# A two-layer kernel: staged first stores, remainders by identity products, attention stacks with spread rows

## The chip, the cores and the metric

The kernel runs on one core of a Trainium2 chip, in one launch. The time is that of the device, in microseconds, for one execution; the median over several runs is compared. The core has a matmul engine (PE, TensorE, with its weight loads PEld), a vector engine (DVE), an activation engine (ACT), a general engine (POOL) and a queue engine for transfers (SP). ACT and POOL can issue transfers too.

## The reference

`x` is (8, 256, 256). Two conditioned residual layers follow each other: `x = x + L0(x)`, then `x = x + L1(x)`.

```
L0: x*s1, layer norm over the channels; q, k, v = projections, each scaled per sample and channel (demodulation)
    16 heads of width 16: softmax(q k^T / 4) v, projected by w; plus v projected by u (skip); all float32
L1: xr, gate = x W_in^T (512 each); xr + t_emb; causal depthwise convolution of 4 taps; silu
    xn = layer norm of 512 channels;  Bm, Cm, dt = xn W_xproj^T (16 each)
    dt = tanh(dt W_dt^T + b_dt) * 0.01;  Ad = 1 - dt*tanh(A_log);  Bd = Bm * min(|xn|, 1)
    256 steps in time: h = clip(h*Ad + Bd x xn, -10, 10);  y = sum over d of C_d h_d
    out = ((y + D*xn) * silu(gate)) W_out^T
```

## The kernel before, in words

Five engine programs are written out by hand; semaphores order them. Every engine works through its own instructions in the order in which they stand, so a wait holds all that stands behind it. SP's queue is in order as well.

**Attention (0 to some 245 us).** Work goes sample by sample. For q and k of a sample PE projects the normalised `xnT` (L940), ACT copies the result to `qk` (L614) and POOL and ACT split it into three bf16 parts (`part`). `stack(b)` on SP (L287 and following) writes the parts of one sample to DRAM by eight transfers (L294) and reads them back as stacks `qst`, `kst` of 96 rows (partitions 0 to 95, by runs of 48, 32 and 16 rows; L307), so that one bf16 matmul of 96 rows gives all needed products of the parts. `max_scores` (L963) makes scores with queries on the partitions, DVE reduces them to row maxima `mx` (L1486), PE turns them round, ACT casts them to `mT` and issues a transfer of one row, `m_row`, into partition 96 of the q stack (L678), where the k stack holds -1. `scores` (L978) then multiplies 97 rows, and gives scores less their maximum, ready for ACT's Exp (L693); `weigh` (L993) multiplies with v. Stacks are in three buffers. PE's `sample(b)` interleaves the scores of sample b, the maxima of b + 1 and the projections of b + 2. Before the loop come the modulated statistics (DVE L1391, L1359), the demodulation sums (PE L924), and sample 0 and 1.

**Middle part (some 245 to 350 us).** Convolution, projections and layer norm statistics of layer 1. Then, for tiles (sample, half of time) in the order FINISHED, the first eight being the first half of each sample: DVE finishes a tile's `xn` by two passes (`centre` L1560, `scale` L1568); ACT casts it to bf16 (`leave_parts` L793); POOL subtracts the cast (`leave_first` L484, into `xrem`); ACT casts the remainder (`second_part` L807); POOL subtracts again into the third part (`leave_second` L490); ACT also squares the tile for the norms (L801). SP stores the parts to `xs_d` (`store_parts` L342). Meanwhile DVE makes the running products of Ad and their inverses (L1619 to L1628), PE turns them round, and `split` (L1635 to L1639) makes three parts of d and, when the norms are there, of B (bsplit). Those go to `bd_d` (`store_d`, `store_b` L263; twelve stores of B over both halves, 32-byte pieces). PE projects the gates 0 to 7 (`project_gate` L1164), ACT takes them through Silu (`take_gate` L765). The first slabs of x parts and B parts are read back into `xst` and `bst` (`load_x` L353, `load_b` L361) by SP, in slabs of 16 time steps, the first slab in two pieces of 8.

**Recurrence (350 us to the end).** 256 steps. PE makes `u` of one step by one bf16 matmul (L1280) in bank t % 4; DVE makes the clipped step by a custom instruction (L1664); PE sums states with C into y (`y_steps` L1291, banks 4 and 5), four steps at a time. Output of a slab, its gate and its projection follow one slab later, and so do the parts of tiles 8 to 15.

## Time and profile before

| | us |
|---|---|
| median of 3 runs (562.87 to 564.33) | 562.97 |
| the profiled execution | 563.17 |
| its span, first to last instruction | 561.4 |
| busy: PE / DVE / ACT / POOL | 471.6 / 430.0 / 253.5 / 194.0 |
| mean granted clock of TensorE | 0.948 |

The page lists what is busy and for how long; the chain of waits follows the work that ended last back through what released it; views by time show one engine's instructions with the idle time before them in brackets and what ended it. PEclk is the granted clock as a share of the full 2.4 GHz, so 0.50 is 1.2 GHz. A float32 matmul stands as two records.

### The profile page before, as it was taken

Reading aid. Unit: us, or ns where it says so; the run is one execution under the profiler, and the core shown is the slowest. Engines: PE = TensorE matmul, PEld = TensorE weight load, DVE = VectorE, ACT = ScalarE, POOL = GpSimd, SP = SyncE. Lnnn points to the kernel's source line nnn. Section 1 sums busy time; section 2 is a strip of 40 time slices with the busy share of each in tenths; the row PEclk is TensorE's granted clock in tenths of the full one; section 3 lists DMA queues with packets and bytes.
Section 4 is the critical chain, followed back from the end, with each engine's and each line's share of the span. In section 5 each row is a group of like instructions: output and inputs, shape, how many; then the busy total and the mean of one; then the engine's idle time right before and its main releaser. Section 6 shows DMA issues by size and latency. Waiting matters only on the chain.

```text
span 561.4 us, 8412 instructions
## 1 busy us (share of the span) xinstructions
PE 471.6 (84%) x3000; PEld 281.7 (50%) x3000; DVE 430.0 (77%) x744; ACT 253.5 (45%) x504; POOL 194.0 (35%) x211
## 2 busy tenths in 40 slices
PE   1958897999999979888999820889999999999996
PEld 1844565667676656567888610123333333333333
DVE  2846353766857676849998982999999999999993
ACT  3322675777576635778667664043221111111111
POOL 6405303023031100000730694079873443343332
PEclk9967898999999999999999875799999999999999
DMA  8884576765847540100065266676545444333310
GB/s 335 320 166 87 85 145 120 139 123 102 166 95 151 112 97 1 39 27 12 0 251 173 94 224 119 205 227 207 189 128 111 127 121 126 121 112 100 100 37 20
DMA packets 44629, 71.80 MB, mean 128 GB/s; under 512 B 18825, under 2 KB 33545, under 8 KB 41468
## 3 DMA queue, kind: packets, MB, share of 16 engines
q1 hardware_dynamic: 40684, 67.55, 45.9%
q0 software_dynamic: 528, 3.55, 1.6%
q10 hardware_dynamic: 3376, 0.16, 0.3%
q8 instruction: 24, 0.39, 0.3%
q14 instruction: 17, 0.14, 0.1%
HBM read 41.88 MB, written 23.02 MB: 116 GB/s over the span
## 4 chain that ended last, share of the span: by engine, by line
PE 49%; DVE 32%; DMA 7%; ACT 5%; issue 4%; POOL 2%; SPq 1%; DVEq 0%; POOLq 0%
DVE win L1664 10%; PE bank L1320 6%; PE bank L1280 6%; PE bank L1291 5%; PE bank L963 5%; PE bank L993 5%; PE bank L940 5%; DVE z L1664 5%; DMA qst<-mT 5%; PE bank L978 4%; PE bank L1042 2%; DVE acc L1464 2%; DVE zlast L1664 2%; DVE lnb_rep L1664 2%; PE bank L1011 2%
## 5 line engine op out<-in xcount | busy, mean ns | idle before, releaser
L1486 DVE TENSOR_REDUCE mx<-bank 128x2 f32<-128x512 f32 x128 | 82.0, 686 | 70.8 <-PE bank L963 70.2
L1280 PE MATMUL bank<-xst,bst 128*128 128x512 bf16 x256 | 82.8, 394 | 39.1 <-DMA bst<-bd_d 23.2
L693 ACT ACTIVATE ex<-bank 128x512 f32<-128x512 f32 x128 | 70.9, 599 | 43.1 <-PE bank L978 43.1
L1664 DVE CUSTOM_DVE_ANT_0 win<-win,bank,hi 128x512 f32<-128x512 f32 x96 | 71.8, 748 | 3.4
L1280 PEld LDWEIGHTS bank<-xst,bst 128*128 128x128 bf16 x256 | 24.9, 98 | 92.8 <-DVE win L1664 30.7
L455 POOL TENSOR_TENSOR qk<-qk,part 128x512 f32<-128x512 f32 x16 | 19.7, 1231 | 128.3 <-ACT part L618 128.3
L978 PE MATMUL bank<-qst,kst 97*128 97x256 bf16 x256 | 46.1, 273 | 10.0 <-DMA qst<-mT 8.3
L963 PE MATMUL bank<-kst,qst 96*128 96x256 bf16 x256 | 49.6, 288 | 5.5 <-DVE mx L1486 5.5
L940 PE MATMUL bank<-xnT,w 128*128 128x256 f32 x192 | 51.9, 428 | 0.8 <-ACT xnT L603 0.7
L563 POOL TENSOR_TENSOR yg<-yT,gateT 128x128 f32<-128x128 f32 x60 | 29.3, 521 | 60.1 <-ACT yT L873 60.1
L865 ACT ACTIVATE ytk<-bank,ybias 128x512 f32<-128x512 f32 x15 | 10.3, 687 | 84.5 <-PE bank L1291 84.5
L940 PEld LDWEIGHTS bank<-xnT,w 128*128 128x128 f32 x192 | 40.9, 220 | 8.2 <-ACT xnT L603 1.7
L1464 DVE SCALAR_TENSOR_TENSOR acc<-xrp,wcv,acc 128x256 f32<-128x256 f32 x96 | 38.6, 476 | 0.8 <-ACT acc L658 0.8
L993 PE MATMUL bank<-ex,vp 128*32 128x256 f32 x512 | 34.3, 385 | 5.5 <-ACT ex L693 5.5
L1320 PE MATMUL bank<-wo,yg 128*128 128x256 f32 x128 | 35.6, 403 | 0.2 <-DVE yg L1675 0.2
L978 PEld LDWEIGHTS bank<-qst,kst 97*128 97x128 bf16 x256 | 22.4, 97 | 26.4 <-DMA qst<-mT 10.3
L1320 PEld LDWEIGHTS bank<-wo,yg 128*128 128x128 f32 x128 | 21.8, 189 | 26.4 <-issue 24.3
L1291 PE MATMUL bank<-win,cst 128*32 128x512 f32 x256 | 35.0, 619 | 0.0
L1291 PE MATMUL bank<-lnb_rep,cst 128*32 128x512 f32 x64 | 33.7, 608 | 1.1 <-DVE zlast L1664 1.1
L1291 PE MATMUL bank<-z,cst 128*32 128x512 f32 x128 | 33.9, 608 | 0.0
L1291 PE MATMUL bank<-zlast,cst 128*32 128x512 f32 x64 | 33.7, 608 | 0.0
L1664 DVE CUSTOM_DVE_ANT_0 win<-zlast,bank,hi 128x512 f32<-128x512 f32 x32 | 23.9, 748 | 12.5 <-PE bank L1280 11.4
(190 smaller groups left out, 906.4 us busy)
## 6 DMA issues: line engine op xcount, KB each, us to landing
qk_d<-part SPq DMA_DIRECT2D x64, 96.0 KB, 2.5
xs_d<-xpart SPq DMA_DIRECT2D x16, 384.0 KB, 4.7
xst<-xs_d SPq DMA_DIRECT2D x15, 384.0 KB
xn_d<-xc SPq DMA_DIRECT2D x16, 256.0 KB, 3.3
xtk<-xn_d SPq DMA_DIRECT2D x64, 64.0 KB
xst<-xs_d SPq DMA_DIRECT2D x15, 256.0 KB
bd_d<-zeros POOLq DMA_DIRECT2D x1, 3468.0 KB, 12.1
qst<-qk_d SPq DMA_DIRECT2D x8, 384.0 KB, 4.5
```

The source lines that it names most:

```text
L563: ins = nc.gpsimd.tensor_tensor(yg[:, c, :].rearrange("p (b g k) -> p b g k", b=B, g=RG), yT[:, c, :].rearrange("p (k g b) -> p b g k", k= ...
L693: nc.scalar.activation(ex[:, n // 4, n % 4, :], bank[6 + n % 2][:, :], ACT.Exp, scale=SCALE)\
L940: ins = mm(bank[bk][:, o * S:(o + 1) * S], w5[:, w, k, o * P:(o + 1) * P], xnT[:, k, :], start=k == 0, stop=k == HT - 1)
L963: ins = mm(bank[4 + n % 2][:, t * S:(t + 1) * S], qstacks[b % NBUF][0:96, STACKED[n], t * P:(t + 1) * P], kstacks[b % NBUF][0:96, STACKED[ ...
L978: ins = mm(bank[6 + n % 2][:, t * S:(t + 1) * S], kstacks[b % NBUF][0:97, STACKED[n], t * P:(t + 1) * P], qstacks[b % NBUF][0:97, STACKED[ ...
L993: ins = mm(bank[par][32 * r:32 * r + 32, o * S:(o + 1) * S], vp[:, b % 2, t, o * (NH // HT) + 4 * par + r, :], ex[:, g, r, t * S:(t + 1) * ...
L1280: mm(bank[t % 4][:, :], bst[:, slot, t % RS, :], xst[slot][:, t % RS, :], start=True, stop=True)\
L1291: ins = mm(bank[4 + i % 2][32 * k:32 * k + 32, :], cst[:, i % 2, 32 * (4 * g + k):32 * (4 * g + k) + 32], zst[(4 * g + k) % ZR], start=g = ...
L1320: ins = mm(bank[7][:, 0:H], yg[:, c, :], wo[:, c, :], start=False, stop=c == CT - 1, skip_group_check=True)
L1464: ins = v.scalar_tensor_tensor(acc[:, b % 2, c, :], xrp[:, b % 2, c, k:k + S], wcv[:, c, k:k + 1], acc[:, b % 2, c, :], ALU.mult, ALU.add)
L1486: v.tensor_reduce(mx[:, :, STACKED[n]:STACKED[n] + 1], bank[4 + n % 2][:, :].rearrange("p (t k) -> p t k", t=HALVES), AX.X, ALU.max)\
L1664: v._custom_dve(bass.dve_ops.TENSOR_ADD_SAT, out=zst[t % ZR], in0=zst[(t - 1) % ZR], in1=bank[t % 4][:, :], s0=hi[:, t:t + 1], s1=0.0).the ...
```

## The change

What it does, part by part:

- **Start.** The first load of x holds two samples. DVE clears the first two q stacks (`qst`, 8192 bf16 elements per partition) before anything else; POOL sets all of `kst` to -1 instead of 32 partitions of it. DVE makes the statistics of sample 1 right behind those of sample 0, of the others after the first demodulation. PE turns sample 1 round before v's projection of sample 0, projects q and k of sample 1 ahead of `v_tokens(0)`; ACT takes them ahead of v of sample 0. Of sample 0's eight stores ACT issues four.
- **Rows spread.** Stack rows go to every second partition: 48 from 0 on, 32 from 63 on, 16 from 1 on; `m_row` goes to partition 127; the matmuls take 127 rows (maxima) and 128 rows (scores). Rows that hold no part are 0 in q and -1 in k. The third buffers are cleared by POOL.
- **Middle, parts.** For the first eight tiles the two remainders are made by PE: identity times the tile, less identity times the cast, in banks 6 and 7. The third part is a cast by DVE. POOL has no part in it. The three parts of d are made in the same way in bank 3. Gates 5 to 7 move behind or between, gate banks change, ACT's Sqrt table is loaded early by a dummy, and gates 5 to 7 are taken behind the first stores of B.
- **Middle, order on DVE.** Tile 1 is finished ahead of `eb_ready`, tiles 2 and 3 ahead of the scan.
- **Stores staged.** Of B's first half and of tile 7, the 16 first time steps are stored first, on semaphores of their own (`bd_first`, `xs_first`), and the first slab's loads wait for these alone; ACT issues four of the six small stores and all six of the rest.

```diff
+STACK_ROWS = ((0, 3), (63, 2), (1, 1))
+M_ROW = P - 1
+def gate_bank(b):
+    return 6 if b in (0, 2, 6) else 4
@@ sync
-                for hh in range(NH // HT): sp.dma_start(qk_d ..., part ...)
+                store_stack(sp, b, range(NH // HT // 2 if b == 0 else NH // HT))
-                    at = 0
-                    for run in (3, 2, 1):
+                    for at, run in STACK_ROWS:
-                        sp.dma_start(st[at:at + run * HD], src.rearrange("k d h s -> (k d) h s"))\
+                        sp.dma_start(st[at:at + 2 * run * HD:2], src.rearrange("k d h s -> (k d) h s"))\
...
             sp.wait_ge(s["bsplit"], 1)
-            store_b(sp, 0, range(3))
-            store_parts(B - 1)
-            parts_stored(B)
+            store_b(sp, 0, range(2), 0, RS, "bd_first")
+            store_parts(B - 1, 0, RS, "xs_first")
+            parts_stored(B - 1)
+            sp.wait_ge(s["xs_first"], 16)
             load_x(0, "ld_xf", 0, FIRST)
-            sp.wait_ge(s["bd_out0"], 16 * 7)
+            sp.wait_ge(s["bd_first"], 16 * 7)
             load_b(0, "ld_bf", 0, FIRST)
             load_x(0, "ld_x0", FIRST)
             load_b(0, "ld_b0", FIRST)
+            store_parts(B - 1, RS, P)
             sp.wait_ge(s["ones_in"], 16)
+            parts_stored(B)
             load_x(1, "ld_x1")
+            sp.wait_ge(s["bd_out0"], 16 * 6)
             load_b(1, "ld_b1")
@@ gpsimd
-            own.mark(nc.gpsimd.memset(kst[96:P, :, :, :], -1.0))
+            nc.gpsimd.memset(kst[:, :, :, :], -1.0).then_inc(s["stacks_clear"], 1)
-            (loop of leave_first, leave_second over eight tiles)
@@ scalar
+            take_xn(1, 0)
+            act.wait_ge(s["part_ready"], 2)
+            store_stack(act, 0, range(NH // HT // 2, NH // HT))
...
+            take_qk(1, 0, 1); take_qk(1, 1, 2); second_cast(1, 0); second_cast(1, 1)
             act.wait_ge(s["dc_done"], 2)
             take_vt(0, 3)
...
+            leave_parts(0); square(0); take_gate(3); leave_parts(1); second_part(0); square(1)
+            leave_parts(2); second_part(1); square(2); leave_parts(3); square(3); take_gate(4)
+            nc.scalar.activation(warm[:, :], ones[:, 0:1], ACT.Sqrt)
+            act.wait_ge(s["eb_back"], 1)
+            split_d(0); (ipct1); second_part(2); (ybias)
+            for j in range(4, B):
+                leave_parts(j)
+                if j < 6:
+                    split_d(j - 3)
+                second_part(j - 1)
+                square(j)
+            (norms by Sqrt); second_part(B - 1)
             act.wait_ge(s["bsplit"], 1)
-            store_b(act, 0, range(3, 6))
+            store_b(act, 0, range(2, 6), 0, RS, "bd_first")
+            take_gate(5)
+            take_gate(6)
+            store_b(act, 0, range(6), RS, P)
+            take_gate(7)
@@ tensor
+            def first_left(j):
+                b, t = FINISHED[j]
+                pe.wait_ge(s["part0"], j + 1)
+                ...
+                mm(bank[6 + j % 2][:, :], ident[:, :], xc[:, b * HALVES + t, :], start=True, stop=False)
+                mm(bank[6 + j % 2][:, :], minus[:, :], xpart[:, j % XRING, 0, :], start=False, stop=True)\
+                    .then_inc(s["rem_ready"], 1)
+            def second_left(j):
+                pe.wait_ge(s["part1"], j + 1)
+                mm(bank[6 + j % 2][:, :], minus[:, :], xpart[:, j % XRING, 1, :], ...).then_inc(s["left_ready"], 1)
+            first_left(0); (turn adt, cdt); first_left(1); second_left(0); second_left(1); project_gate(4)
+            (turn back); first_left(2); (ybias sums); second_left(2); first_left(3); left_of_d(0); project_gate(5, 0, 1)
+            second_left(3); first_left(4); left_of_d(1); second_left(4); first_left(5); project_gate(5, 1, 2)
+            second_left(5); first_left(6); second_left(6); first_left(7); project_gate(5, 2, 3); second_left(7)
             project_gate(5, 3, 4); project_gate(6); project_gate(7)
...
             u_steps(0)
-            pe.wait_ge(s["gate_out"], B)       (now ahead of the first y_steps, behind u_steps(1))
@@ vector
+            v.memset(qst[:, :, :, :], 0.0).then_inc(s["stacks_clear"], 1)
             dve.wait_ge(s["ld_first"], 32)
+            (statistics, roots and normalise of sample 0, then of sample 1; demodulate q, k)
             modulated_statistics(2 * HALVES, NT)
...
+            def last_part(j):
+                dve.wait_ge(s["left_ready"], j + 1)
+                v.tensor_copy(xpart[:, j % XRING, 2, :], bank[6 + j % 2][:, :]).then_inc(s["parts_ready"], 1)
+            last_part(0); finish((4,)); last_part(1); finish((5,)); last_part(2); finish((6,))
+            last_part(3); finish((7,)); last_part(4); last_part(5); last_part(6)
             (norms, B, split(bpart, ...))
+            last_part(7)
+            finish(range(8, IN_FRONT))
```

## Rows read from the trace of the kernel before

**Rows 1.** The chain of waits in order of time: start us, us, what

```profile
36.71 7.55 PE bank L940 x24
...
57.89 7.85 DMA qst<-mT
...
82.19 6.06 DMA qst<-mT
...
339.14 4.80 DMA xs_d<-xpart
```

**Rows 2.** PE by time: start, us, line, out<-in, count [idle before <-releaser]

```profile
44.09 0.60 PE L963 MATMUL bank<-kst,qst 96*128 96x256 bf16 x4
...
65.79 0.61 PE L978 MATMUL bank<-qst,kst 97*128 97x256 bf16 x4 [2.60 <-DMA qst<-mT]
...
88.29 0.61 PE L978 MATMUL bank<-qst,kst 97*128 97x256 bf16 x4 [3.09 <-DMA qst<-mT]
...
349.48 2.53 PE L1280 MATMUL bank<-xst,bst 128*128 128x512 bf16 x5 [23.25 <-DMA bst<-bd_d]
```

**Rows 3.** The waits: waiter <- releaser: us in total, times, longest

```profile
PE bank L978 <- DMA qst<-mT: 8.3, 5, 3.1
```

**Rows 4.** SP's queue by time: DMAs issued, count

```profile
27.11 3.76 SPq L294 DMA_DIRECT2D qk_d<-part  x8
...
34.23 1.35 SPq L307 DMA_DIRECT2D kst<-qk_d  x3
...
78.23 1.36 SPq L307 DMA_DIRECT2D kst<-qk_d  x3
...
335.65 3.45 SPq L263 DMA_DIRECT2D bd_d<-bpart  x3
...
344.09 2.18 SPq L353 DMA_DIRECT2D xst<-xs_d  x3
```

**Rows 5.** POOL by time

```profile
0.73 6.92 POOL L440 MEMSET kst<- 32x8192 bf16 x1 [0.29 <-POOLq L1717]
```

**Rows 6.** DVE by time, in the middle part

```profile
303.33 0.42 DVE L1602 TENSOR_TENSOR dtt<-dtt,proj_off 128x256 f32<-128x256 f32 x1
...
303.67 0.68 DVE L1603 TENSOR_TENSOR raw<-raw,rs 128x512 f32<-128x512 f32 x1
...
332.36 1.28 DVE L1650 TENSOR_TENSOR bnt<-raw,nrm 128x128 f32<-128x128 f32 x1
```

**Rows 7.** ACT by time, its queue's DMAs (ACTq) too

```profile
40.53 0.84 ACT L614 ACTIVATE qk<-bank,dc 128x256 f32<-128x256 f32 x2 [3.87 <-PE bank L940]
...
64.74 1.28 ACT L693 ACT_TABLE_LOAD   x1
...
335.70 2.44 ACTq L263 DMA_DIRECT2D bd_d<-bpart  x3
```

**Rows 8.** Stretches of the span: granted clock and DMA rate behind PEclk

```profile
core 0: us, PE busy (x) PEld busy (x) DVE busy (x) ACT busy (x) POOL busy (x), PEclk, DMA share, GB/s
14.00:18.00 4.00, 4.00 (x15) 3.64 (x16) 1.36 (x8) 0.23 (x1) 0.00 (x0) 1.00 1.03 441
...
34.00:38.00 4.00, 3.26 (x11) 2.68 (x12) 1.70 (x8) 1.23 (x2) 0.00 (x0) 0.50 1.04 203
...
314.00:318.00 4.00, 4.00 (x11) 3.20 (x12) 4.00 (x6) 3.03 (x7) 2.38 (x2) 0.57 0.17 68
```

**Rows 9.** Groups from 300 to 345 us by shape: busy us, mean ns

```profile
L1164 PE MATMUL bank<-xres,win 128*128 128x256 f32 x92 | 22.1, 402 | 0.0
...
L484 POOL TENSOR_TENSOR xrem<-xc,xpart 128x512 f32<-128x512 f32 x10 | 12.9, 1295 | 33.5 <-ACT xpart L793 33.0
...
L490 POOL TENSOR_TENSOR xpart<-xrem,xpart 128x512 bf16<-128x512 f32 x9 | 12.2, 1357 | 0.1
...
L1568 DVE SCALAR_TENSOR_TENSOR xc<-xc,rs,lnr 128x512 f32<-128x512 f32 x12 | 12.2, 1053 | 0.1
...
L807 ACT ACTIVATE xpart<-xrem 128x512 bf16<-128x512 f32 x10 | 6.2, 623 | 1.1 <-POOL xrem L484 0.9
```

More of the change, by code:

```diff
@@ L262, in store_b, with store_stack @@
                 rows = rows.rearrange("b (t c) -> t b c", c=P)[:, :, 0:NS]
[L263 to L264 removed]
+                eng.dma_start(rows[t * P + lo:t * P + hi],
+                              bpart[lo:hi, PAIRS[j][1], t, :].rearrange("p (b d) -> p b d", b=B))\
+                   .then_inc(s[done or f"bd_out{t}"], 16)
+        def store_stack(eng, b, which):
+            for hh in which:
+                eng.dma_start(qk_d[b % 2, :, :, :, hh * HT:(hh + 1) * HT, :].rearrange("w k d h s -> d (w k) (h s)"),
+                              part[hh * HD:(hh + 1) * HD, :, :, :].rearrange("p w k s -> p (w k) s"))\
+                   .then_inc(s["pw"], 16)
         block = ctx.enter_context(nc.Block())
@@ L806, in second_part @@
                 act.wait_ge(s["rem_ready"], j + 1)
-                nc.scalar.activation(xpart[:, j % XRING, 1, :], xrem[:, j % 2, :], ACT.Copy).then_inc(s["part1"], 1)
+                left = bank[6 + j % 2][:, :] if j < B else xrem[:, j % 2, :]
+                nc.scalar.activation(xpart[:, j % XRING, 1, :], left, ACT.Copy).then_inc(s["part1"], 1)
             for b in range(B):
@@ L821, in _, with split_d @@
                     last_tap(b + 2)
-            act.wait_ge(s["rt_in"], 5)
+            act.wait_ge(s["rt_in"], 6)
             nc.scalar.activation(rt[:, :], var_e[:, :], ACT.Sqrt).then_inc(s["rt_out"], 1)
+            take_gate(2)
             act.wait_ge(s["dt_in"], 1)
             nc.scalar.activation(dtt[:, :, :], dtt[:, :, :], ACT.Tanh).then_inc(s["dt_out"], 1)
-            take_gate(2)
-            for j in range(B):
+            def split_d(k):
+                if k == 0:
+                    act.wait_ge(s["eb_back"], 1)
+                else:
+                    act.wait_ge(s["d_left"], k)
+                nc.scalar.activation(dpart[:, k, 0, :], bank[3][:, 0:P], ACT.Copy)\
+                    .then_inc(s["dsplit" if k == 2 else "d_part"], 1)
@@ new lines, in _ @@
+            leave_parts(0)
+            square(0)
+            take_gate(3)
+            leave_parts(1)
+            second_part(0)
+            square(1)
+            leave_parts(2)
+            second_part(1)
+            square(2)
+            leave_parts(3)
+            square(3)
+            take_gate(4)
+            nc.scalar.activation(warm[:, :], ones[:, 0:1], ACT.Sqrt)
+            act.wait_ge(s["eb_back"], 1)
+            split_d(0)
+            nc.scalar.activation(ipct1[:, :, :], bank[0][:, 0:2 * P].rearrange("p (k c) -> p k c", k=2), ACT.Copy)\
+                .then_inc(s["ipct_ready"], 1)
@@ L1178, in _ @@
             style_sums((2, 3, 4), 5)
+            transpose_xn(1, 0)
             channels_of(2, 3, "vt_done")
@@ L1191, in _ @@
             channels_of(1, 2, "k_done")
+            v_tokens(0)
             pe.wait_ge(s["v_in"], 1)
```

225 lines of the change are left out of this document (125 added, 100 removed).

## The prediction

> **What bounds the kernel now.** I read the page first: PE is busy 84% of the span, DVE 77%, and the 40 slices show one hole, around slices 23 to 25, where PE falls to 2 and 0 tenths. Then the chain of waits, in order of time, which cuts the span in three.
>
> Attention, up to about 245 us, is mostly PE, but with waits of its own. The chain passes through the small DMA that puts a sample's negated maxima into the last stack row: 7.85 us for sample 0, 6.06 for sample 1 [rows 1], for 8 KB. PE stood idle 2.60 us and 3.09 us before these two samples' scores [rows 2], 8.3 us in all over five samples [rows 3]. The reason is read from SP's queue: sample 2's six stack loads were issued up to 79.6 us [rows 4], 1.5 MB, and the small DMA issued at 82.19 landed at 88.25, behind them. Sample 0's was issued at 57.89, when sample 1's loads had just been issued.
>
> The middle part, from the last statistics (301 us) to the first matmul of the recurrence (349.48 us, after 23.25 us of idle PE [rows 2]), is a chain through POOL (the two subtractions per tile), a wait of DVE for the norms at 332.1, the split of B, three stores of B by SP, the store of tile 7's parts (4.80 us, landed 343.96 [rows 1]) and the first loads, which SP starts at 344.09 [rows 4].
>
> The recurrence, from 349.48 on, is DVE's custom steps one after another, 0.78 us apart, 256 of them: the rest of the span, 211.9 us, changes only where a load is late.
>
> **Start: memset, bigger first load.** DVE's new memset writes 8192 elements per partition. The trace has no such DVE row. POOL's of 8192 elements took 6.92 us [rows 5]; two DVE tensor_tensor rows, 0.42 us for 256 and 0.68 us for 512 elements [rows 6], give 1.02 ns per element, 8.3 us. An instruction that does two elements per cycle would give half, 4.2 us. I take 8.3, as DVE's own nearest row: it ends at about 9.1 us, where the first statistics began at 7.49 behind the broadcast load. The 256 KB more in the first load, at between 203 and 441 GB/s [rows 8], are 0.6 to 1.3 us, to 8.8 us at most. So everything at the start moves by 1.6 us, at least 0.8. The Trainium skill ("VectorE: DVE Perf Modes", "Zero memsets can be issued as uint32 (trn2)") says that a memset takes one cycle per element whatever the type, which at its 0.96 GHz would be, as an estimate, 8.5 us, and half if it is issued at 4 bytes; no row of this trace shows either, and the sum would move by 0.2 us or by -0.8 us.
>
> **Start: second sample sooner.** Before, DVE did the statistics of 14 tiles (from 18.28 to 28.5) before sample 1 was normalised, and PE's 24 projections of it ran 36.71 to 44.26 at half clock [rows 1]. Now DVE does two tiles in the 4.5 us in which it waited for the style sums, so this is free. ACT's first projection copy of sample 1 (40.53 before [rows 7]) then waits for sample 0's stores instead. Those: parts ready at 27.1 + 1.6 = 28.7; ACT first copies the second sample (behind v's projection, to 29.6), then issues four stores. Eight took SP 3.76 us, 0.47 each [rows 4]; four at 0.5 to 0.8 us on ACT end at 31.6 to 32.8, and landing takes 2.1: 34.2 against 32.94. From the copy to part_ready of sample 1 it was 7.0 us (40.53 to 47.53), so 41.2 instead of 47.5, and its loads are issued by 49.6 instead of 55.9. What is now late: v_tokens(0) waits for ACT, which takes v only after sample 1's casts (39.5 to 40.4), then v_in, then four projections: PE is free at 44 to 45, and sample 0's maxima begin there, against 44.09 [rows 2]. I take +0.4 us. The maxima themselves are DVE's reductions, unchanged, 12.6 us.
>
> At 58.3 the small DMA of sample 0 meets empty queues and takes about 3.3 us instead of 7.85. PE's projections of sample 2 end at 63.2 + 0.4, so PE gains 2.2 us; but ACT is the next late one: its table load for Exp stood at 64.74 to 66.02 [rows 7], behind two copies which wait for these projections. So the first exponential gains nothing, and PE only catches up in the sample: I take 1.3 of the 2.60 us. Start in all: +0.4 - 1.3 = -0.9.
>
> **Rows spread.** Stack rows go to partitions 0, 2, .. 94, 63, 65, .. 125 and 1, 3, .. 31. While stacks load, the DMA engines are busy 1.04 of the time at 203 GB/s; the same share gave 441 GB/s while 128-partition tensors came in [rows 8]. So it is the destination or the short spans that cost, and there is room: bounds are no gain and 2.2 times. Against DRAM-side costs, which do not change, I take 1.4 times: 8 us of loads become 5.7. Then sample 1's small DMA lands by about 85 and nearly all of its 3.09 goes (2.8), and of the 2.6 that three later samples lost (8.3 - 2.60 - 3.09), 2.1. At no gain, these 4.9 us are nothing. Matmuls over 127 or 128 rows instead of 96 or 97 cost what their 256 columns cost: 0. Spread: -4.9.
>
> Here the Trainium skill ("SBUF — State Buffer", "Door 1: The DMA port swizzle") has a rule that half supports the edit: partitions 0 to 63 reach only 8 of 16 ports. Old rows put 64 of 96 on them, new ones 49. By its table 1 MiB into 0..63 goes at 196 GB/s, which the 203 agrees with. But it also says that only one transfer that spans all 128 partitions uses all ports, and each new transfer spans two thirds or less. By that the gain in rate would be under 1.3 and the sum up to 2 us later.
>
> **Middle: parts by PE.** A tile costs POOL 1295 + 1357 ns [rows 9], up to 1.6 us each while DVE's two passes (1053 ns mean [rows 9], 0.7 alone) share with it. New per tile: ACT three passes of about 0.55 plus the read of the accumulator, 1.8 us; DVE two passes of 0.68 and one cast from a bank of 0.65, 2.0 us; PE a float32 identity product of 512 columns, 2 x 0.43 us (two records of 0.216 us per 256 columns at full clock), and two bf16 products of 0.22, 1.3 us. Worked through in order: the first tile is scaled at 304.4 (305.0 before), tile 1 at 305.8, but eb_ready comes at 308.2 (306.6 before) and ipc_ready at 315.0 (312.9), as two finishes stand ahead of each; that is the price of the move, 2.1 us for the B and d chain. ACT meets gate 4 at 315.9 to 317.0, a table load to 318.3 (1.28, now off the end), and then tiles 2 to 7 follow at about 2.1 us: cast 2 at 319.8, 3 at 322.2, 4 at 324.7, 5 at 326.6, 6 at 328.8, norms at 329.8, cast 7 at 330.7. B: 1.28 us for the product of 128 elements [rows 6] was beside POOL and becomes 0.4; with the split of 1.6, bsplit is at 332.4 and parts_ready(8) at 333.0, against 335.6 and 335.7. At 1.2 GHz the PE part doubles to 2.6 us a tile. The clock fell to 0.57 at 314 to 318, after PE had been half idle [rows 8], and PE has such gaps again at 308 to 312; I add 1 us: 333.4. A gain of 2.2.
>
> **Middle: staged stores.** Before, from bsplit: 3.45 us for SP's three stores of B [rows 4], 0.7 issue and 4.80 landing of tile 7, then 5.4 to the first matmul: 13.9 us. Now SP issues two stores of 16 rows (at most 1.1 each, I take 0.5), then 48 KB of tile 7, landing 2.4 as the smallest stores did, then 5.4 again: 333.4 + 1.0 + 0.5 + 2.4 + 5.4 = 342.7; ACT's four beside it, at 0.81 (2.44 for three [rows 7]) end at 336.7 and land in time. First matmul 342.7 against 349.48: -6.8, of which 4.6 are here. Bounds: with issues of 1.15 us and the full 4.8, 346.4; with none of the 1 us for the clock, 341.7.
>
> **Tail of the gates and the second slab.** ACT after its four stores: table load 1.28, gate 5 to 339.1, gate 6 to 340.2, six stores of the other rows (0.81 to 1.15 each) to 345 to 347, gate 7 to 348. PE does gate 7 from 339.1 for 3.5 us: it ends at 342.6, as the loads land. y_steps(0, 0) waits for gate 7 at 348, and DVE's eight first steps last until 350: hidden by 1 us, if the clock is full. Then load_x(1) waits for tile 7's store behind four loads, issued 344.4, landing 349; load_b(1) for the six stores, landing 350 to 352; it arrives at 355 to 356, and step 16 wants it at 355.8. Cover gone by a little: +1.0 us (0 to 3).
>
> **Sum.** -0.9 - 4.9 - 6.8 + 1.0 = -11.6 from the profiled execution's 563.2 (span 561.4 and 1.8 around it, 0.2 over the median of 563.0): 551.6.
>
> **Rivals.** (1) Spread rows load no faster: 551.6 + 4.9 = 556.5. For it: each DMA still spans a part of the partitions. Against: 441 GB/s beside 203. (2) The small stores and the ACT queue are slow: six stores at 1.6 us put gate 7 to 351 and load_b(1) to 359, 3.5 us of stall instead of 1.0, and first loads 2 us later: 556. For it: 896 pieces of 32 bytes per store. (3) Better: full clock, no stall, first loads right behind, and 2 us more in attention as ACT is less late: 546. (4) Slower: PE stays at 1.2 GHz through the whole middle part. Then it is the bound: eight tiles x 2.6, four gates x 6.9 (L1164, twice the 0.216 us per record of full clock) and some 3 us of gaps make 51 us from 306, first matmul at 357.5, 8 us later than before; with -5.8 of attention and +1 it is 566. It is slower than before once that first matmul is behind 354.3. Against it: clock 1.00 came back by 318 as soon as gates ran. (5) The staging does not shorten anything, as the loads wait for some other store: first matmul 347, 556.
>
> **Numbers.** Forecast (548 to 554.5) 0.52; (1) 0.15; (2) and (5) 0.13; (3) 0.09; (4), with anything else of that sign, 0.11. A change of under 0.3%, 1.7 us, can't be told from none. Faster 0.86, same 0.03, slower 0.11. Range 545 to 559: all cases but (4) and the ends.
>
> **What would show it.** Sample 0's small DMA under 4 us and PE idle before L978 under 2.5 us in all; GB/s over 260 in stack loads; ACT's Exp table load within 0.5 us of 64.7; bsplit at 333.4; first u matmul at 342 to 344; one stall of DVE at step 16. Wrong it would be with PEclk at 0.5 over most of 306 to 340, or with DVE gaps of over 3 us in the first three tiles of the recurrence.

## The result, and the profile after

The changed kernel takes 548.61 us in the median of 4 runs (547.81 to 549.44); the kernel before, on the same chip, took 563.65 us (562.87 to 567.17, 4 runs). The ratio is 0.9716, with a 95% interval of 0.9677 to 0.9756. The forecast was 551.6 (545 to 559). The profiled execution took 549.22 us with a span of 547.4; before it was 563.2 with 561.4. So the 14.0 us between the spans are what has to be explained. All ratios here and below are of fast runs; the one slow run, the 550.88 us of a_all, stands in its median and not in its ratio.

I cut both spans at three rows: the last statistics (`var_e`), the last cast of B's split, and the first matmul of the recurrence (u1).

| stretch | before | after | difference | forecast |
|---|---|---|---|---|
| start and attention, to `var_e` | 300.92 | 293.88 | -7.04 | -5.8 |
| `var_e` to the split of B | 34.69 | 30.47 | -4.22 | -2.2 |
| split of B to u1 | 13.87 | 11.29 | -2.58 | -4.6 |
| u1 to the end | 211.92 | 211.76 | -0.16 | +1.0 |

**Attention.** ACT's queue of the changed kernel by time, with the small DMA of each sample's maxima (start us, us to issue, what):

```profile
57.68 0.60 ACTq L691 DMA_DIRECT2D qst<-mT  x1
81.08 0.53 ACTq L691 DMA_DIRECT2D qst<-mT  x1
103.76 0.51 ACTq L691 DMA_DIRECT2D qst<-mT  x1
...
217.60 0.53 ACTq L691 DMA_DIRECT2D qst<-mT  x1
```

The last of the kernel before's eight; the starts of its first two are in [rows 1], 57.89 and 82.19:

```profile
224.64 0.51 ACTq L678 DMA_DIRECT2D qst<-mT  x1
```

At sample 0 the two differ by 0.21 us, at sample 7 by 7.04: the maxima of sample 0 are not ready sooner, and the gain came between the samples (0.9 us in the first gap, 2.78 in the second, whose end was at 107.65 before). The largest of PE's idle times of [rows 2] and [rows 3], in the changed kernel (waits: waiter <- releaser: us in total, times, longest; then PE by time):

```profile
PE bank L1020 <- DMA qst<-mT: 2.0, 1, 2.0
```

```profile
62.89 0.60 PE L1020 MATMUL bank<-qst,kst 128*128 128x256 bf16 x4
...
86.08 0.61 PE L1020 MATMUL bank<-qst,kst 128*128 128x256 bf16 x4 [1.98 <-DMA qst<-mT]
```

8.3 us of PE's waiting are down to 2.0. Sample 0's scores begin 2.9 us sooner, behind the projections with no wait; sample 1's still wait. The cause is in the DMA view (DMA issues: KB each, median us from issue to landing), before and then after:

```profile
kst<-qk_d SPq DMA_DIRECT2D x8, 384.0 KB, 7.8
...
kst<-qk_d SPq DMA_DIRECT2D x8, 128.0 KB, 8.8
qst<-mT ACTq DMA_DIRECT2D x8, 8.0 KB, 3.5
```

```profile
kst<-qk_d SPq DMA_DIRECT2D x8, 384.0 KB, 5.5
...
kst<-qk_d SPq DMA_DIRECT2D x8, 128.0 KB, 5.5
...
qst<-mT ACTq DMA_DIRECT2D x8, 8.0 KB, 1.8
```

With the same bytes in the same number of transfers, the `kst` loads, which are issued last, land 1.4 to 1.6 times as fast; the `qst` loads ahead of them gain less (384 KB in 3.9 us instead of 4.5, 128 KB in 4.6 instead of 5.9). Sample 0's small DMA took 1.9 us instead of 7.85, so nothing held it up; sample 1's, issued at 81.08 behind sample 2's loads, still took 4.95.

**Middle.** Stretches of the changed kernel (the number ahead of DMA share and GB/s is the granted clock; columns as in [rows 8]):

```profile
310.00:314.00 4.00, 2.21 (x36) 1.42 (x25) 3.74 (x6) 2.97 (x9) 0.00 (x0) 1.00 0.80 284
...
330.00:334.00 4.00, 2.41 (x12) 1.77 (x10) 0.25 (x1) 0.86 (x2) 0.00 (x0) 1.00 0.96 150
334.00:338.00 4.00, 2.19 (x5) 0.64 (x6) 1.62 (x3) 4.00 (x8) 0.37 (x1) 0.56 0.72 173
```

PE kept the 2.4 GHz level (1.00) from `var_e` to about 334.5, where before it had a mean of 0.57 in one stretch [rows 8]. POOL is idle from 310 to 334. A tile in PE's order, and then ACT's casts of two (both of the changed kernel, by time):

```profile
314.17 0.39 PE L1300 MATMUL bank<-xpart,minus 128*128 128x512 bf16 x1
314.40 1.02 PE L1293 MATMUL bank<-xc,ident 128*128 128x512 f32 x2
315.26 0.38 PE L1294 MATMUL bank<-xpart,minus 128*128 128x512 bf16 x1
...
316.55 0.39 PE L1300 MATMUL bank<-xpart,minus 128*128 128x512 bf16 x1 [0.86 <-ACT xpart L828]
```

```profile
318.05 0.60 ACT L828 ACTIVATE xpart<-bank 128x512 bf16<-128x512 f32 x1 [0.43 <-PE bank L1294]
...
320.20 0.60 ACT L828 ACTIVATE xpart<-bank 128x512 bf16<-128x512 f32 x1 [0.43 <-PE bank L1294]
```

A tile is a closed round of 2.15 to 2.4 us: PE makes the first remainder (L1293, L1294), ACT waits for it and casts it (L828), PE waits for the cast to subtract it (L1300), and only then takes the next tile. Neither engine is full; the round is. The product with the norms, 1.28 us beside POOL [rows 6], takes 0.29 with POOL idle:

```profile
322.09 0.29 DVE L1758 TENSOR_TENSOR bnt<-raw,nrm 128x128 f32<-128x128 f32 x1
```

Not all of this stretch's gain has to come from PE's remainders. ACT's share of the middle changed as well: the kernel before takes gates 5 to 7 between its tiles and loads Sqrt's table right before the norms (one gate and the load below, by time); the changed kernel takes these gates behind the split and loads the table at 309.32, ahead of the last tiles.

```profile
326.27 1.09 ACT L765 ACTIVATE gateT<-bank 128x512 f32<-128x512 f32 x2 [0.72 <-PE bank L1164]
...
329.25 1.28 ACT L844 ACT_TABLE_LOAD   x1
```

From `var_e` to ACT's last root of the norms it took 31.0 us before (331.92) and 27.6 now (321.44). POOL was busy 3.77 to 3.95 of each 4 us from 318 to 330 before, so POOL and ACT were both near their limits. No kernel here moves the gates and the table load alone, or the remainders alone; how the 4.2 us divide between them is open.

**First loads.** SP's queue, ACT's queue and the chain of waits of the changed kernel, from the split of B on:

```profile
324.38 0.80 SPq L271 DMA_DIRECT2D bd_d<-bpart  x2
325.23 0.42 SPq L357 DMA_DIRECT2D xs_d<-xpart  x1
329.08 2.17 SPq L368 DMA_DIRECT2D xst<-xs_d  x3
```

```profile
324.44 1.78 ACTq L271 DMA_DIRECT2D bd_d<-bpart  x4
...
328.84 0.92 ACTq L271 DMA_DIRECT2D bd_d<-bpart  x2
...
329.79 3.31 ACTq L271 DMA_DIRECT2D bd_d<-bpart  x4
```

```profile
325.23 3.46 DMA xs_d<-xpart
...
332.07 3.05 DMA bst<-bd_d
```

```profile
335.64 2.08 PE L1371 MATMUL bank<-xst,bst 128*128 128x512 bf16 x4 [3.23 <-DMA bst<-bd_d]
```

From the split to SP's first load it is 4.73 us (before 8.5), but from there to u1 it is 6.56 (before 5.39, from [rows 4] and [rows 2]). ACT's six stores of the other rows, issued from 328.84 to 333.10, run beside these loads: DMA share 0.96 at only 150 GB/s in 330 to 334. The clock fell at about 334.5, when PE had been idle since 332.4, and u1 ran at the lower level.

### The profile page after: what moved, and what is told of

It is laid out like the page before. It is cut to its first block, busy times and chain, and to the rows that moved or that the text cites. A ratio compares the mean times of both kernels' runs of the same rounds, so it can differ in the third digit from the quotient of the medians.

```text
span 547.4 us, 8477 instructions
## 1 busy us (share of the span) xinstructions
PE 473.7 (87%) x3014; PEld 282.7 (52%) x3034; DVE 431.0 (79%) x754; ACT 254.9 (47%) x510; POOL 174.5 (32%) x196
## 4 chain that ended last, share of the span: by engine, by line
PE 53%; DVE 31%; ACT 6%; DMA 4%; issue 3%; SPq 1%; POOL 0%; ACTq 0%; DVEq 0%
DVE win L1773 11%; PE bank L982 7%; PE bank L1411 6%; PE bank L1035 5%; PE bank L1371 5%; PE bank L1382 5%; DVE z L1773 5%; PE bank L1005 5%; PE bank L1020 4%; PE bank L1084 3%; PE bank L1062 3%; DVE acc L1561 3%; DVE zlast L1773 2%; DVE lnb_rep L1773 2%; PE bank L1209 2%
## 5 line engine op out<-in xcount | busy, mean ns | idle before, releaser
L1371 PE MATMUL bank<-xst,bst 128*128 128x512 bf16 x238 | 78.3, 394 | 21.8 <-DVE win L1773 8.8
L1005 PE MATMUL bank<-kst,qst 127*128 127x256 bf16 x256 | 48.1, 280 | 6.2 <-DVE mx L1583 5.6
L982 PE MATMUL bank<-xnT,w 128*128 128x256 f32 x192 | 50.4, 418 | 0.9 <-ACT vp L651 0.8
L1020 PE MATMUL bank<-qst,kst 128*128 128x256 bf16 x256 | 46.1, 273 | 5.4 <-ACT ex L706 3.2
L982 PEld LDWEIGHTS bank<-xnT,w 128*128 128x128 f32 x192 | 39.3, 212 | 7.7 <-ACT vp L651 1.2
L1020 PEld LDWEIGHTS bank<-qst,kst 128*128 128x128 bf16 x256 | 22.5, 97 | 21.3 <-ACT ex L706 10.5
L1005 PEld LDWEIGHTS bank<-kst,qst 127*128 127x128 bf16 x256 | 22.4, 98 | 19.7 <-DVE mx L1583 16.6
```

Source lines behind the costliest of these rows:

```text
L982: ins = mm(bank[bk][:, o * S:(o + 1) * S], w5[:, w, k, o * P:(o + 1) * P], xnT[:, k, :], start=k == 0, stop=k == HT - 1)
L1005: ins = mm(bank[4 + n % 2][:, t * S:(t + 1) * S], qstacks[b % NBUF][0:M_ROW, STACKED[n], t * P:(t + 1) * P], kstacks[b % NBUF][0:M_ROW, ST ...
L1020: ins = mm(bank[6 + n % 2][:, t * S:(t + 1) * S], kstacks[b % NBUF][:, STACKED[n], t * P:(t + 1) * P], qstacks[b % NBUF][:, STACKED[n], :] ...
L1371: mm(bank[t % 4][:, :], bst[:, slot, t % RS, :], xst[slot][:, t % RS, :], start=True, stop=True)\
```

## The experiments

Twelve kernels, in three groups, each group on one chip with the kernel before. "Before plus" kernels add parts to the kernel before; "after" kernels alter the changed one. The stretches are those of the table above, from each one's profile.

| kernel | to `var_e` | to split | to u1 | to end | median us | ratio to before [95%] |
|---|---|---|---|---|---|---|
| b_rows | 294.49 | 34.71 | 14.10 | 211.50 | 556.19 | 0.985 [0.9794, 0.9906] |
| b_rows_start | 294.45 | 34.69 | 14.44 | 211.52 | 556.34 | 0.9844 [0.9782, 0.9906] |
| b_rows_start_stage | 295.82 | 34.73 | 10.21 | 211.54 | 553.09 | 0.9787 [0.9722, 0.9853] |
| b_stage | 304.02 | 34.71 | 10.44 | 211.03 | 561.13 | 0.9933 [0.9902, 0.9963] |
| a_packed | 298.71 | 30.47 | 10.23 | 211.49 | 553.88 | 0.9804 [0.9764, 0.9844] |
| a_twice | 293.08 | 34.06 | 11.24 | 211.52 | 552.27 | 0.9776 [0.9747, 0.9805] |
| a_late_rest | 293.34 | 30.48 | 9.57 | 211.61 | 546.42 | 0.9684 [0.9645, 0.9723] |
| a_ld_act | 296.70 | 30.48 | 9.73 | 211.09 | 549.72 | 0.9713 [0.9669, 0.9757] |
| a_same | 293.31 | 30.47 | 11.36 | 211.06 | 549.45 | 0.9738 [0.9712, 0.9764] |
| a_order | 292.20 | 31.11 | 11.33 | 211.56 | 549.35 | 0.9739 [0.9708, 0.9771] |
| a_exp | 293.00 | 30.48 | 11.39 | 211.53 | 548.80 | 0.9717 [0.9676, 0.9758] |
| a_all | 291.42 | 31.11 | 10.15 | 211.12 | 548.38 | 0.9706 [0.9655, 0.9757] |

The median of before was 565.11 for the first four, 564.99 for the next four and 563.94 for the last four. The first column moves by itself from one execution to the next: the attention code is the same in the changed kernel, a_same, a_twice, a_late_rest, a_ld_act and a_order, and it reads 292.2 to 296.7; that of before and b_stage is the same too, and reads 300.9 and 304.0. The second column repeats within 0.05 us for the same code. The third reads 10.2 to 11.4 for the same stores. So single profiles decide for the middle and the recurrence, but not for a term of one or two microseconds in the attention, nor for one of under 1.2 from the split to u1 as a whole.

One source of the differences is TensorE's clock at about 58 us, where the copies that ACT waits for come from 16 projections. Stretch 58 to 60 and the projections, in before and in b_rows:

```profile
58.00:60.00 2.00, 2.00 (x6) 1.55 (x6) 0.07 (x1) 0.00 (x0) 0.00 (x0) 0.50 1.03 164
...
57.53 5.65 PE L940 MATMUL bank<-xnT,w 128*128 128x256 f32 x16
```

```profile
58.00:60.00 2.00, 2.00 (x10) 1.74 (x9) 0.00 (x0) 0.09 (x1) 0.00 (x0) 0.91 1.02 258
...
57.42 4.18 PE L944 MATMUL bank<-xnT,w 128*128 128x256 f32 x16
```

PE had been granted 1.2 GHz (0.50) while it waited for DVE's maxima, and where it comes back to 2.4 GHz within these projections decides 1.5 us: a_twice and a_late_rest have it early (0.66 and 0.70), the changed kernel and a_same, with the same code, late (0.50). The last number of the first two rows is the loads' rate as well: 164 GB/s with packed rows, 258 with spread ones.

**b_rows**: before plus the spread rows and their memsets.

```
+STACK_ROWS = ((0, 3), (63, 2), (1, 1))
-sp.dma_start(st[at:at + run * HD], ...)
+sp.dma_start(st[at:at + 2 * run * HD:2], ...)
-act.dma_start(qstacks[b % NBUF][96:97], mT[:, :])
+act.dma_start(qstacks[b % NBUF][M_ROW:P], mT[:, :])
... (memsets of qst by DVE and kst by POOL; matmuls over 127 and 128 rows)
```

> The kernel before with one part of the change alone: stack rows spread over every second partition, negated maxima in partition 127, with the clearing that this needs (all of kst by POOL, qst by DVE at the start). Start order, middle part and stores as before. Theory A (the attention part's 7.0 us come from stack loads that finish sooner, so that the one-row transfers no longer queue behind them): the last statistics (var_e, 300.9 before) at 294.5 to 296, PE's idle time before the scores for the one-row transfer falls from 8.3 to under 2.5 us, the span from 561.4 to 555 to 557. Theory B (it is sample 1's earlier start that empties the queues, the spread does little): idle time still 7 to 8 us, span 560 to 562.

It shortens the attention by 6.4 us and nothing else; up to 1.5 us of them may be the early clock of the row above. PE's idle time for the small DMA fell from 8.3 to 3.3 us, not to under 2.5 as expected: sample 0's wait of 2.60 us is down to 0.90 without any new start, but sample 1's is still 2.39. Its median is 1.5% below before; the changed kernel's is 2.8% below.

**b_rows_start**: b_rows plus the new order of the start.

```
-for dst, src in ((xt[:, 0:HALVES, :], x_tok[:, 0:HALVES, :]),
+for dst, src in ((xt[:, 0:2 * HALVES, :], x_tok[:, 0:2 * HALVES, :]),
...
+take_xn(1, 0)
+act.wait_ge(s["part_ready"], 2)
+store_stack(act, 0, range(NH // HT // 2, NH // HT))
```

> The kernel before with spread rows and the new start (second sample sooner, four of sample 0's stores on ACT). Theory A: the start adds little, var_e at 293.9 as in the changed kernel, 0.5 to 1.5 us less than with the rows alone; span 554 to 554.7. Theory B: 5 us less than with the rows alone.

294.45 against 294.49, and medians 0.15 us apart: on top of spread rows, the new start gives nothing that shows, where 0.5 to 1.5 us were expected (b_rows_start had the late clock, 0.50 in 58 to 60, so up to 1.5 us may be hidden in this). PE's idle time for the small DMA did fall, from 3.3 to 1.7 us. ACT of the changed kernel in sample 0:

```profile
63.09 0.84 ACT L627 ACTIVATE qk<-bank,dc 128x256 f32<-128x256 f32 x2 [0.46 <-PE bank L982]
...
64.61 1.28 ACT L706 ACT_TABLE_LOAD   x1
```

Sample 1's loads start at 45.37 instead of 53.27, and PE's scores of sample 0 at 62.89 instead of 65.79, but ACT loads the table at 64.61 (64.74 before [rows 7]) behind two copies of sample 2's projections. The 7.9 us on the queue and the 2.9 us of PE end as 0.13 us of ACT.

**b_rows_start_stage** and **b_stage**: the staged stores, on top of b_rows_start, and on the kernel before alone.

```
-store_b(sp, 0, range(3))
-store_parts(B - 1)
-parts_stored(B)
+store_b(sp, 0, range(2), 0, RS, "bd_first")
+store_parts(B - 1, 0, RS, "xs_first")
+parts_stored(B - 1)
...
+store_b(act, 0, range(2, 6), 0, RS, "bd_first")
+store_b(act, 0, range(6), RS, P)
```

> The same with the staged first stores too; the middle's parts still by POOL, gates where they were. Against the changed kernel only the identity products with their new order are missing. Theory A (parts 4.2 us, staging 2.6 us, they add up): var_e to the end of B's split takes 34.7 us as before, from there to the first matmul of the recurrence 11 instead of 13.9, span 551 to 552. Theory C (staging only pays as the new middle leaves the queues free; with POOL's late last parts the stores wait for parts of tile 7 anyway): no gain over the kernel without it, span 554 or more.

> The kernel before with the staged first stores alone. Theory A: the first matmul of the recurrence at 346 to 347 instead of 349.5, span 558 to 559.5. Theory C: within 0.5 us of 561.4. In both nothing changes before 335 us.

The stretch from the split to u1 fell from 14.44 to 10.21 and from 13.87 to 10.44, so staging is worth 3.4 to 4.2 us with the old middle part; that it would pay only with the new one is refuted. Both kernels had 10.2 to 10.4 us there, and so did a_packed, with the changed kernel's stores (10.23); the changed kernel and four others with its stores had 11.2 to 11.4. The difference is taken up below. The span of b_rows_start_stage, 552.3, was just over the 551 to 552 expected. That of b_stage, 560.2, was over its 558 to 559.5, because in that execution the last statistics stood at 304.0, 3 us later than in before's profile, in code that is the same; its ten runs put it 0.7% under before. Its own row, the landing in the chain of waits, against 4.80 in [rows 1]:

```profile
340.10 2.25 DMA xs_d<-xpart
```

**a_packed**: the changed kernel with its stack rows side by side again.

```
-STACK_ROWS = ((0, 3), (63, 2), (1, 1))
+STACK_ROWS = ((0, 3), (48, 2), (80, 1))
-sp.dma_start(st[at:at + 2 * run * HD:2], ...)
+sp.dma_start(st[at:at + run * HD], ...)
```

> The changed kernel with the stack rows side by side again (partitions 0 to 95); all else, the row 127 too, as in it. Theory A (loads are limited by where they write): last of a stack's six loads lands some 2 us later, PE waits again for the one-row transfer of the samples from 1 on, 4 to 5.5 us in all; var_e from 293.9 to 298 to 299.5; span 551.5 to 553. Theory B (the start's order does it): within 1 us of 547.4.

4.8 us of the 7.0 are lost, and the landing times of before and most of its waits are back (DMA issues, then the waits, of a_packed):

```profile
kst<-qk_d SPq DMA_DIRECT2D x8, 128.0 KB, 8.7
qst<-mT ACTq DMA_DIRECT2D x8, 8.0 KB, 3.1
```

```profile
PEld bank L1020 <- DMA qst<-mT: 7.6, 5, 3.8
PE bank L1020 <- DMA qst<-mT: 5.2, 2, 3.4
```

The size is that of single profiles: 298.71 stands 2.0 to 6.5 us above the readings of the changed kernel's attention code. The sign is safe, since it is above all six of them, and the ratio's interval, 0.9764 to 0.9844, doesn't meet that of the changed kernel, 0.9677 to 0.9756. The other 2.2 us, with the start as the main other edit ahead of `var_e`, are no more than this spread. The waits say more: start and spread rows overlap, as each alone relieves sample 0's small DMA (it has 0.90 us of wait left in b_rows and none in a_packed, where it landed in 1.9 us), and together they can free it only once. The number of rows, the bytes and the matmuls are those of the changed kernel; only the partitions of the loads' rows differ. So it is where the rows lie, not how they are split into transfers. Whether it is the wider range of partitions or the step of two isn't separated.

**a_twice**: the changed kernel with a second float32 identity product of each tile, overwritten by the one that counts.

```
+mm(bank[6 + j % 2][:, :], ident[:, :], xc[:, b * HALVES + t, :], start=True, stop=True)
```

> The changed kernel with every identity product of the first eight tiles issued twice into the same bank (the second overwrites the first), so PE has 0.86 us more per tile. As forecast (ACT with 1.8 and DVE with 2.0 us per tile set the pace, PE has 1.3 and slack): at most 1 us later in all. Rival, read from the trace of the changed kernel, where ACT waits for PE in the last tiles (cast of the remainder, second product, next identity product, next cast follow each other): a serial round through PE, ACT and PE, so each of the last five or six tiles costs 0.86 us more, B's split ends 4 to 5 us later, span 551.5 to 552.5.

The middle grew by 3.59 us, from 30.47 to 34.06. PE of a_twice by time:

```profile
314.38 0.39 PE L1301 MATMUL bank<-xpart,minus 128*128 128x512 bf16 x1
314.61 1.02 PE L1293 MATMUL bank<-xc,ident 128*128 128x512 f32 x2
315.46 1.02 PE L1294 MATMUL bank<-xc,ident 128*128 128x512 f32 x2
316.32 0.38 PE L1295 MATMUL bank<-xpart,minus 128*128 128x512 bf16 x1
...
317.62 0.39 PE L1301 MATMUL bank<-xpart,minus 128*128 128x512 bf16 x1 [0.86 <-ACT xpart L828]
```

The round went from 2.38 us (314.17 to 316.55 above) to 3.24 (314.38 to 317.62), by the 0.86 us of the added product, and PE's idle time in it stayed 0.86. The last four rounds, from 314.38 to 326.66, each took 0.86 us more than those of the changed kernel (314.17 to 323.02), 3.4 of the 3.59 us; ahead of them the extra products cost next to nothing. That is less than the rival's 4 to 5 us for five or six tiles, and far from the 1 us at most of the forecast. In these rounds PE had idle time and yet no slack: its work and ACT's cast follow each other.

**a_late_rest** and **a_ld_act**: the changed kernel with ACT's stores of the other rows behind gate 7, and with the two loads of B's first rows issued by ACT instead of SP.

```
-store_b(act, 0, range(6), RS, P)
 take_gate(7)
+store_b(act, 0, range(6), RS, P)
```

```
+act.wait_ge(s["bd_first"], 16 * 7)
+load_b(act, 0, "ld_bf", 0, FIRST)
... (on SP: all six first loads of x ahead of the loads of B that are left)
```

> The changed kernel with ACT's six stores of the other 112 rows of B moved behind gate 7. Theory D (from the landing of tile 7's rows to the first matmul it took 6.56 us instead of 5.4, as these stores' 32-byte pieces share the DMA engines with the first loads): first matmul 0.8 to 1.2 us sooner, 334.6, and the second slab still in time; span 546.2 to 546.7. Rival (the six DMAs that SP issues one after another set it, not their sharing): first matmul within 0.3 us of 335.64, span 547.4, or later if the second slab is late.

> The changed kernel with the first two loads of B's parts issued by ACT, behind gate 5, beside SP's three of x, instead of behind them. If SP's issue of five loads in a row sets the first matmul (3.7 us from 329.08): first matmul 1.3 to 2 us sooner, at 333.7 to 334.3, span 545.5 to 546. If the sharing of the DMA engines sets it: within 0.4 us of 335.64. PE ends gate 7 at 332.4, so it can't be much sooner than 333.

Split to u1 came to 9.57 and 9.73 instead of 11.3. PE of a_late_rest by time; SP had issued its first load at 327.71:

```profile
333.39 0.81 PE L1371 MATMUL bank<-xst,bst 128*128 128x512 bf16 x3 [1.50 <-DMA bst<-bd_d]
```

From the first load's issue to u1 it is 5.68 us (5.93 in a_ld_act, 6.50 in a_same, 6.56 in the changed kernel). So 0.8 to 0.9 us of the 1.7 in a_late_rest are the stores beside the loads. Issuing from ACT (a_ld_act) gives 0.6 there, less than the 1.3 to 2 us that its expectation had for SP's issue as the limit; that the whole 1.6 met it is luck. The rest stands ahead of SP's loads: 3.89 us from the split in a_late_rest and 3.80 in a_ld_act, 4.73 and 4.86 in the changed kernel and a_same. Their spans, 545.0 and 548.0, missed what was expected (546.2 to 546.7, 545.5 to 546), one each way, by the attention's spread and this part. It is set by tile 7's landing, 2.61 us in a_late_rest against 3.46, at a time when the moved stores have not been issued; the edits don't explain it, and 3.67 in a_packed, with the stores where they were, says that it changes between executions. What sets it is open.

**a_same**, **a_order**, **a_exp**, **a_all**: the changed kernel's code again, as a base on the same chip; the first remainder of tile j+1 put ahead of the second of tile j from tile 2 on; Exp's table loaded ahead of the sample loop; and a_late_rest, a_ld_act, a_order and a_exp together.

```
 first_left(j + 1)
-second_left(j)          # stood ahead of first_left(j + 1)
+second_left(j)
```

```
+nc.scalar.activation(warm[:, :], ones[:, 0:1], ACT.Exp)
```

> The changed kernel once more, unchanged, beside the three that follow: what its parts vary by between executions. All theories: from the last statistics to B's split 30.5 us within 0.1, the recurrence 211.0 to 211.8; var_e 293 to 297 and the way from the split to the first matmul 10 to 11.5 us, as both hang on transfers from DRAM.

> The changed kernel with PE's order turned in the tile part: the next tile's identity product ahead of this tile's second product. Theory (a serial round cast, second product, next identity product, next cast of 2.15 us per tile sets the pace): the round is cut, ACT's 1.8 and DVE's 2.0 us per tile are next, last statistics to B's split 29.2 to 29.8 instead of 30.48. Rival (PE's own work or ACT's sets the pace): 30.3 to 30.6.

> The changed kernel with a dummy Exp of one column on ACT ahead of sample 0, so that the table of Exp is loaded while ACT is idle (46 to 56 us) and not at 64.6. Theory (the second sample's earlier start brought nothing, since ACT's copies and this load stand ahead of the first exponential): from sample 0's one-row transfer to sample 1's 22.1 us instead of 22.0 to 23.4, that is 0.8 to 1.3 us less than beside it in the unchanged one, the span by as much. Rival (PE's work in the sample is the limit): less than 0.3 us.

> The changed kernel with all of it: PE's order turned, Exp table early, first loads of B's parts by ACT, six other stores of B behind gate 7. If the four add up: split 0.7 to 1.3 sooner, first matmul 9.2 us behind it or less, 0 to 1.2 us in attention; span 543 to 545. If the second slab comes late as a price (gap of DVE at step 16): 1 to 2 us of it are lost.

a_order should have opened the round and gained 0.7 to 1.3 us; it lost 0.64, outside its rival's range as well. PE of a_order by time:

```profile
313.86 1.10 PE L1293 MATMUL bank<-xc,ident 128*128 128x512 f32 x2 [0.82 <-DVE xpart L1741]
...
318.67 1.10 PE L1293 MATMUL bank<-xc,ident 128*128 128x512 f32 x2 [0.88 <-DVE xpart L1741]
```

There are two banks for the tiles, so the product of tile j+1 then waits until DVE has cast tile j-1 out of its bank. The wait for ACT has become a wait for DVE, and two tiles take 4.81 us (313.86 to 318.67), 2.40 each.

a_exp took the table load away, and the first exponential began 6.9 us after the issue of sample 0's small DMA, not 8.2 as in the changed kernel: the second small DMA went out 22.07 us after the first, not 23.24 as in a_same. But the third then came after 24.44 us instead of 22.50. PE's wait for the second is not the reason, 2.07 us against 1.81 in a_same. The granted clock is: behind that wait it was 0.55 and 0.60 in 84 to 88 in a_exp and 1.00 in a_same, and the next eight projections took 3.38 us instead of 1.89, 1.5 of the 1.9 us (PE by time, a_exp and then a_same):

```profile
84.59 3.38 PE L983 MATMUL bank<-xnT,w 128*128 128x256 f32 x8
```

```profile
86.24 1.89 PE L982 MATMUL bank<-xnT,w 128*128 128x256 f32 x8
```

`var_e` is 293.00 against 293.31. That ACT was late is shown; whether an earlier start of ACT is worth anything at the end is open, as no run shows what a_exp gives when the clock stays up.

a_all took 10.15 us from the split to u1, 1.2 less than a_same, where 9.2 or less was expected, and lost 0.64 in the middle, where 0.7 to 1.3 were to be gained. Behind SP's first load it had 5.37 us against 6.50, more than either edit on the loads saved alone. Its ratio, 0.9706, and a_same's, 0.9738, have intervals that overlap: no difference that these runs can tell. a_late_rest has the lowest median, 546.42, but was timed on another chip than a_same, and the intervals of their ratios overlap. No kernel here is shown to beat the changed one.

## Why the prediction was right, by its steps

- **The bound** was read rightly: the small DMA behind the stack loads, the POOL chain, and three serial trips through DMA before the recurrence. All three moved, and the recurrence stayed at 211.0 to 211.9 us in all kernels, before and after.
- **Spread rows, -4.9**: measured 4.8 when taken back (a_packed), which is how the step counted it, with the start in place; -6.4 when done alone (b_rows), sample 0's wait and the early clock being in that. With a spread of 4.5 us between readings of the same attention code, that 4.8 meets 4.9 so closely is luck; the sign and the rough size are shown. The `kst` loads landed 1.4 times as fast for the large transfer, as taken, and 1.6 for the small one. Rival (1), no faster, is out, and so is the gain in rate of under 1.3 that the step worked out beside its own; its premise that no new transfer spans more than two thirds of the partitions was wrong too, as the largest goes from 0 to 94, 95 of 128.
- **Start, -0.9**: -2.2 by a_packed against before, about 0 by b_rows_start against b_rows, both within what the same code varies by; its size isn't known. The two attention terms came to -7.0 together against -5.8. Inside the start two things were off. The memset was mis-sized, 8.3 us from two DVE rows with float32 operands; it ran in 3.47, as 4-byte elements:

```profile
1.65 3.47 DVE L1497 MEMSET qst<- 128x4096 uint32 x1 [1.65 <-PEq L1826]
7.76 0.76 DVE L1483 TENSOR_TENSOR xt<-xt,s1b 128x256 f32<-128x256 f32 x2 [2.64 <-DMA s1b<-s_row]
```

  It was done before the broadcast load came, so the start moved by 0.27 us (7.49 before), not 1.6. And PE's gain in sample 0 was cut as the step said, by ACT's table load; what a_exp gained there was lost again at the next sample, to a slower clock.
- **Parts by PE, -2.2**: -4.2, 2.0 us too little, in two places. I added 1 us for a slow clock; PE kept the upper level from 306 to 334. And of the rest, 32.5 - 1.0 = 31.5 us forecast from `var_e` to the split against 30.47 measured; 0.7 of this was there already when ACT had loaded Sqrt's table (16.7 us behind `var_e`, forecast 17.4). The working took the pace from sums of each engine's work; in the last tiles the pace is the round through PE, ACT and PE, which is by luck of the same size, about 2.2 us. a_twice shows it: "PE 1.3 us a tile" beside ACT's 1.8 looked like slack, and each added 0.86 us came out in full in the last four rounds. The matched middle times (`ipc_ready` 13.89 us after `var_e`, forecast 14.1) say that the price of two finishes ahead of the B and d chain was right.
- **Staged stores, -4.6**: -2.6 in the changed kernel, -3.4 to -4.2 with the old middle, where tile 7's rows landed in 2.13 and 2.25 us. Two terms of the sum were short: issue and landing of tile 7's rows, taken as 0.5 + 2.4, were 3.46, with 0.39 more to SP's next load; from load to matmul, taken as the 5.4 of before, was 6.56. Of this second one a_late_rest shows 0.8 to 0.9 us to be ACT's six other stores beside the loads. The forecast has these stores from 340.2 on and its first matmul at 342.7, so it had the overlap in its own times and put it at nothing, without a reason. They came sooner too: their first was issued 4.5 us behind the split, forecast 6.8, as ACT's four stores ahead of them took 1.78 us and not 3.3. The later four took 0.83 us each, as in the forecast. The sum of before was also misread: 0.7 us of issue is part of the 4.80 of landing, and 3.45, 0.7, 4.80 and 5.4 make 14.4, not 13.9. Rival (5) is out, since SP's first load moved 3.8 us nearer to the split.
- **Second slab, +1.0**: nothing. ACT's early stores are the reason. The last of the six was issued 2.5 us ahead of u1; the forecast had it 2.3 to 4.3 us behind. SP issued the second slab's loads of x 3.8 us and of B 5.8 us behind u1 (339.46 and 341.47), and step 16 began at 349.31 without a wait. Rival (2) needed 1.6 us a store, which didn't come; its other half, first loads 2 us later than forecast, did.
- **Rival (4)**, PE at 1.2 GHz in the middle part, was wrong in its condition: from 306 to 334 the granted clock was 1.00 even where PE was busy 2.2 us of 4. The half clock came at about 334.5, ahead of u1, and stood to 342 at least; DVE has one gap of 0.50 us there, as before.
- **The signs**: sample 0's small DMA took 1.9 us (under 4), PE's waits were 2.0 us (under 2.5), the table load stood at 64.61 (64.7). The rate of the stack loads was 229 to 295 GB/s in the stretches of 2 us that they fill, 256 in the mean, where over 260 was asked; before it was 180 to 188. The split (333.4) and u1 (342 to 344) were given without the attention's gain; with its -5.8 they are 327.6 and 336.2 to 338.2, against 324.35 and 335.64. The stall at step 16 didn't come.

The sum was 2.4 us above the profiled execution (549.22), and that is a net of errors of both signs: attention 1.2, the middle 2.0 and the recurrence 1.2 too high, the first stores 2.0 too low. That the middle and the stores cancelled is luck. The places where the time was lost were read rightly. Two mechanisms were not: what sets the pace of the tiles, and the stores that run beside the first loads.

## What to carry to other kernels

When small DMAs wait behind large loads, look at the rate of the large ones: here a destination on every second partition instead of side by side cut the landing of the last loads from 8 or 9 to 5.5 us with not one byte less. Idle time of an engine in a chain is not slack; follow one tile through the engines and add the round before you price extra work on any of them, and count the buffers before you reorder it. Price what will run beside a load, not only what stands ahead of it. And time that a queue or one engine gains early in a loop must be followed to the next engine that is late: in the start, 7.9 us on a queue became 0.13 us of ACT. Compare the clock of two profiles before you explain what differs between them.

## What the runs showed of the hardware that I had not expected

- A DVE memset of 128x8192 bf16 zeros ran as 128x4096 uint32 in 3.47 us, 0.85 ns for each 4-byte element, less than the 1.02 ns per element of the DVE rows that the forecast went by. The Trainium skill ("VectorE: DVE Perf Modes", "Zero memsets can be issued as uint32 (trn2)") says that such a memset can be issued at 4 bytes; the trace agrees, 4096 elements being recorded. Half of the 8.5 us that the prediction estimated from that section would be 4.3; the row has 3.47, and the measurement decides.
- Loads to every second partition land faster (8.8 to 5.5 us for 128 KB behind two larger ones) but take longer to issue: three on SP's queue took 1.77 us, side by side 1.25.
- Small pieces went with busy DMA engines and a low rate: 150 GB/s at a share of 0.96 while B's first loads and ACT's stores of 32-byte pieces ran together, where the stack loads of before had 203 GB/s at 1.04 [rows 8].
- The same DVE product of 128 x 128 float32 took 1.28 us where POOL was busy and 0.29 where it was idle, 4.4 times. It began at 332.36, just behind a POOL subtraction, and ended at 333.64, 0.15 us behind its end (POOL of the kernel before, by time):

```profile
332.34 1.15 POOL L484 TENSOR_TENSOR xrem<-xc,xpart 128x512 f32<-128x512 f32 x1
```

  In b_rows and b_stage it is the same, 1.28 us with an end 0.2 us behind that of a POOL subtraction. So these rows read as DVE waiting for POOL's instruction to end; no run tests it.
- The same attention code took from 292.2 to 296.7 us to the last statistics in single profiled executions, in part by where the granted clock came back (sixteen projections 4.2 to 5.8 us) or, in a_exp, fell (eight projections 3.38 us instead of 1.89); terms below 2 us there can't be read from one profile.
